# Attention score matmuls of 16 heads on two row halves of TensorE, and the order of the side rounds

## The reference

```python
qkv = (x @ w_qkv).reshape(b, s, 3, 16, 16)            # 16 heads of width 16
q, k, v = jnp.moveaxis(qkv, 2, 0)
attn = softmax(einsum('bqhd,bkhd->bhqk', q, k) * 16 ** -0.5)
x = layernorm(x + einsum('bhqk,bkhd->bqhd', attn, v).reshape(b, s, d) @ w_proj + b_proj)
# mixture of 8 experts, top 2, capacity 5120 rows: x -> (gelu(x W1a) * (x W1b)) W2, gated, summed by token
x = layernorm(x + experts(x))
```

## Time and profile before

| | us |
|---|---|
| median of 3 runs | 3741.0 (3740.78 to 3743.41) |
| profiled execution, its span | 3738.5 |
| PE busy | 3498.9 (94%) |
| DVE busy | 2507.9 (67%) |
| ACT busy | 2007.2 (54%) |
| POOL busy | 1171.2 (31%) |

### The profile page before, as it was taken

How to read it: one execution, slowest core, us unless ns; L and a number is a source line. 1 busy time by engine, 2 the same in 40 slices (tenths; PEclk the granted TensorE clock), 3 DMA queues, 4 the chain that set the end, 5 groups by cost and what they waited for, 6 DMA issues and landing times. The chain is left out here.

```text
span 3738.5 us, 68180 instructions
## 1 busy us (share of the span) xinstructions
PE 3498.9 (94%) x19714; PEld 2455.3 (66%) x19714; DVE 2507.9 (67%) x5866; ACT 2007.2 (54%) x3877; POOL 1171.2 (31%) x929
## 2 busy tenths in 40 slices
PE   5999999999999999999999968999999999999970
PEld 3555565555555555555556537888888888888860
DVE  6787787777778778778777745455555545454539
ACT  2666666666666666666666653444444444444420
POOL 3013213122131231221312233343444535353334
PEclk8999999999999999999999989999999999999985
DMA  6777777756565555555555624444434443443439
GB/s 114 153 156 158 167 151 172 128 92 106 87 107 93 93 105 88 95 104 92 106 91 91 105 71 78 62 75 69 63 64 63 74 64 62 60 68 50 57 56 337
DMA packets 410259, 376.39 MB, mean 101 GB/s; under 512 B 249528, under 2 KB 311360, under 8 KB 409920
## 3 DMA queue, kind: packets, MB, share of 16 engines
q1 hardware_dynamic: 346944, 287.82, 41.5%
q0 software_dynamic: 58368, 67.74, 11.5%
q10 hardware_dynamic: 4608, 16.78, 1.1%
HBM read 89.92 MB, written 152.17 MB: 65 GB/s over the span
## 5 line engine op out<-in xcount | busy, mean ns | idle before, releaser
L880 DVE TENSOR_REDUCE peak<-ps_rows 128x1 f32<-128x512 f32 x2048 | 1349.7, 681 | 477.8 <-PE ps_rows L557 460.9
L648 ACT ACTIVATE probs<-ps_cols 128x512 f32<-128x512 f32 x2048 | 1120.5, 600 | 378.5 <-PE ps_cols L566 375.2
L557 PE MATMUL ps_rows<-stack 128*128 128x512 f32 x2048 | 893.8, 438 | 46.5 <-issue 33.3
L1088 PE MATMUL ps_hid<-x_hi,stack 128*128 128x512 f32 x2560 | 804.6, 395 | 33.0 <-DVE x_lo L1181 28.4
L566 PE MATMUL ps_cols<-stack 128*128 128x512 f32 x2048 | 813.1, 398 | 2.3 <-ACT probs L648 1.9
L1058 POOL DMA_INDIRECT x<-out,token x320 | 503.6, 1574 | 797.7 <-ACT out L1144 657.6
L1187 DVE TENSOR_TENSOR hid<-ps_hid,act_in 128x512 f32<-128x512 f32 x320 | 218.8, 688 | 599.0 <-ACT act_in L1130 598.8
L557 PEld LDWEIGHTS ps_rows<-stack 128*128 128x128 f32 x2048 | 389.6, 190 | 309.7 <-DVE peak L880 213.5
L1088 PEld LDWEIGHTS ps_hid<-x_hi,stack 128*128 128x128 f32 x2560 | 476.6, 189 | 142.5 <-DVE x_lo L1181 28.5
L579 PE MATMUL ps_pv<-probs,v 128*17 128x512 f32 x4096 | 545.1, 604 | 0.9 <-ACT probs L648 0.9
L423 POOL TENSOR_SCALAR var_eps<-mv 128x4 f32<-128x4 f32 x32 | 7.5, 234 | 1593.9 <-DVE mv L752 1593.9
(11 more groups left out here) (130 smaller groups left out, 3575.5 us busy)
## 6 DMA issues: line engine op xcount, KB each, us to landing
stack<-qk_hi SPq DMA_DIRECT2D x512, 128.0 KB
stack<-qk_lo SPq DMA_DIRECT2D x512, 128.0 KB
expert_rows<-blank SPq DMA_DIRECT2D x80, 520.0 KB, 5.0
quarters<-expert_rows SPq DMA_DIRECT2D x320, 128.0 KB, 2.7
xs<-in_L_attn_x SPq DMA_DIRECT2D x32, 512.0 KB, 3.4
x<-row SPq DMA_DIRECT2D x32, 512.0 KB
fy<-x SPq DMA_DIRECT2D x32, 512.0 KB, 4.7
out<-fz ACTq DMA_DIRECT2D x32, 512.0 KB, 4.9
```

What stands on the lines that cost most here:

```text
L557: pe.matmul(ps_rows[n % ROWS][:], q_stack[s][:, h, t * P:(t + 1) * P], k_stack[s][:, h, :], start=True, stop=True).then_inc(s_rows, 1)
L648: act.activation(probs[:, j % RING, :], ps_cols[j % 2][:], ACT.Exp, scale=SCALE).then_inc(s_exp, 1)
L880: dve.tensor_reduce(peak[s % 2][:, j:j + 1], ps_rows[n % ROWS][:], AX.X, ALU.max, negate=True).then_inc(s_max, 1)
L1088: last = pe.matmul(ps_hid[f % 2][:, part, :], w[c.par][:, k, cols], xx[c.odd][:, k, :], start=i == 0, stop=i == 3 * KT - 1)
```

## The change

The score operands lie in two row halves of 64 rows: even heads in one, odd heads in the other. Each half holds three terms (the lo.lo product is dropped), 48 rows, and two rows for the maxima. A unit's row score reads one half and its column score the opposite one. The four units between two pv now follow each other: all rounds stand directly behind a pv (j = 1, 5, 9, 13), several of them in one place where needed. DVE's side work is moved to match.

```diff
-STACK = 4 * HD
+TERMS = 3
+STACK = TERMS * HD
 AUG = 2
+HALF = P // 2
+PAIRS = HG // 2
 ROUNDS = [
-    (0, 1, "x1T0", -2), (0, 3, "x1T1", -2), (0, 5, "peak3", -1), (0, 7, "turn1", -1), (0, 9, "xT0", 1),
-    (0, 11, "logit", -2), (0, 13, "xT1", 1), (0, 15, "logitT", -2),
-    (1, 3, "qk0", 1), (1, 5, "peak0", 0), (1, 7, "turn2", -1), (1, 11, "qk1", 1), (1, 15, "qk2", 1),
-    (2, 1, "place", -2), (2, 3, "qk3", 1), (2, 5, "peak1", 0), (2, 7, "turn3", -1), (2, 11, "oT0", -1), (2, 13, "oT1", -1),
-    (2, 15, "proj0", -1),
-    (3, 3, "proj1", -1), (3, 5, "peak2", 0), (3, 7, "turn0", 0), (3, 11, "v0", 1), (3, 15, "v1", 1),
+    (0, 1, "xT0", 1), (0, 1, "xT1", 1), (0, 5, "peak3", -1), (0, 5, "turn1", -1), (0, 9, "x1T0", -2),
+    (0, 9, "x1T1", -2), (0, 13, "logit", -2),
+    (1, 1, "logitT", -2), (1, 1, "qk0", 1), (1, 5, "peak0", 0), (1, 5, "turn2", -1), (1, 9, "qk1", 1), (1, 13, "qk2", 1),
+    (2, 1, "place", -2), (2, 1, "qk3", 1), (2, 5, "peak1", 0), (2, 5, "turn3", -1), (2, 9, "v0", 1), (2, 13, "oT0", -1),
+    (2, 13, "oT1", -1),
+    (3, 1, "proj0", -1), (3, 5, "peak2", 0), (3, 5, "turn0", 0), (3, 9, "proj1", -1), (3, 13, "v1", 1),
 ]
+def rows_unit(j):
+    return 1 - j % 2, j // (2 * TILES), j % (2 * TILES) // 2
...
-                        for r, (a, c) in enumerate([(hi, hi), (lo, hi), (hi, lo), (lo, lo)]):
-                            rows = slice(HD * r, HD * r + HD)
...
-                        sp.dma_start(q_stack[g][STACK:STACK + AUG].bitcast(F32), zero_rows[:]).then_inc(s_stack[g], 16)
+                        for half_ in range(2):
+                            part = slice(first + half_ * (GP // 2), first + (half_ + 1) * (GP // 2))
+                            for r, (a, c) in enumerate([(hi, hi), (lo, hi), (hi, lo)]):
+                                rows = slice(HALF * half_ + HD * r, HALF * half_ + HD * (r + 1))
...
-                        sp.dma_start(q_stack[g][STACK:STACK + AUG].bitcast(F32), peak_rows[g % 2][:]).then_inc(s_aug[g], 16)
+                        for half_ in range(2):
+                            rows = slice(HALF * half_ + STACK, HALF * half_ + STACK + AUG)
+                            sp.dma_start(q_stack[g][rows].bitcast(F32),
+                                         peak_rows[g % 2][half_ * UNITS:(half_ + 1) * UNITS]).then_inc(s_aug[g], 16)
...
-                            pe.matmul(ps_rows[n % ROWS][:], q_stack[s][:, h, t * P:(t + 1) * P],
-                                      k_stack[s][:, h, :], start=True, stop=True).then_inc(s_rows, 1)
+                            half_, h, t = rows_unit(j)
+                            part = slice(HALF * half_, HALF * half_ + STACK)
+                            pe.matmul(ps_rows[n % ROWS][:], q_stack[s][part, h, t * P:(t + 1) * P],
+                                      k_stack[s][part, h, :], start=True, stop=True).then_inc(s_rows, 1)
...
-                            pe.matmul(ps_cols[j % 2][:], k_stack[g][:, h, t * P:(t + 1) * P], q_stack[g][:, h, :],
+                            t, h, half_ = j // HG, j % HG // 2, j % 2
+                            part = slice(HALF * half_, HALF * half_ + STACK + AUG)
+                            pe.matmul(ps_cols[j % 2][:], k_stack[g][part, h, t * P:(t + 1) * P], q_stack[g][part, h, :],
                                       start=True, stop=True).then_inc(s_cols, 1)
...
-                        if j:
-                            empty(s, j - 1)
+                        for name in AT[s, j - 1] if j else []:
+                            empty(name)
...
-                        if j in (8, 9) and it.on(-1 if s < 3 else 0):
-                            (turn_sums if j == 8 else turn)(f"turn{(s + 1) % 4}", (s + 1) % 4)
-                        low = {(1, 5): 0, (1, 13): 1, (2, 0): 2, (2, 5): 3}
+                        if j in (6, 7) and it.on(-1 if s < 3 else 0):
+                            (turn_sums if j == 6 else turn)(f"turn{(s + 1) % 4}", (s + 1) % 4)
+                        low = {(1, 3): 0, (1, 11): 1, (1, 15): 2, (2, 3): 3}
...
-                        if it.on(1) and s == 0 and j in (11, 15):
-                            low_x((j - 11) // 4)
+                        if it.on(1) and s == 0 and j in (3, 4):
+                            low_x(j - 3)
```

More of the change, by code:

```diff
@@ L63 @@
 OFFSET = {r[2]: r[3] for r in ROUNDS}
-AT = {(r[0], r[1]): r[2] for r in ROUNDS}
+AT = {(s, j): [r[2] for r in ROUNDS if r[:2] == (s, j)] for s in range(4) for j in range(UNITS)}
+def rows_unit(j):
+    return 1 - j % 2, j // (2 * TILES), j % (2 * TILES) // 2
 def wait(engine, sem, value):
@@ L155, with __init__ @@
 class Weights:
-    def __init__(self, stacks, probs, w1, w2):
+    def __init__(self, stacks, w2_buf, probs, w1, w2):
         flat = [stack[:].rearrange("p h n -> p (h n)") for stack in stacks]
         half = FT * DIM
-        self.w1_hi, self.w1_lo = [[flat[i + j].rearrange("p (k f) -> p k f", k=KT) for j in range(2)] for i in (0, 2)]
-        self.w2_hi, self.w2_lo = [[flat[4 + j][:, i * half:(i + 1) * half].rearrange("p (k d) -> p k d", k=FT)
+        self.w1_hi, self.w1_lo = [[flat[i + j:i + j + KT] for j in (0, 2 * KT)] for i in (0, KT)]
+        self.w2_hi, self.w2_lo = [[w2_buf[:, 2 * j + i].rearrange("p (k d) -> p k d", k=FT)
                                    for j in range(2)] for i in range(2)]
@@ L402, in _ @@
             for g in range(GROUPS):
[L404 to L413, removed]
+                for half_ in range(2):
+                    rows = slice(HALF * half_ + 32, HALF * half_ + HALF)
+                    if g + half_ == 0:
+                        pool.wait_ge(s_blank, 2)
+                    else:
+                        pool.wait_ge(s_pad, 2 * g + half_)
+                    pool.memset(k_stack[g][rows].bitcast(F32), 1.0).then_inc(s_pad, 1)
+            pool.wait_ge(s_pad, 2 * GROUPS)
             pool.wait_ge(s_weights, 64)
@@ L581, in body @@
                                 last.then_inc(s_pv, 1)
-                        name = AT.get((s, j))
-                        if name and it.on(OFFSET[name]):
-                            round_(it, name)
+                        for name in AT[s, j]:
+                            if it.on(OFFSET[name]):
+                                round_(it, name)
             iterations(pe, n_seq, body)
@@ L598, in copy_out, with empty @@
                     act.copy(out, in_).then_inc(s_free[it.bank(name)], 1)
-                def empty(s, j):
-                    name = AT.get((s, j))
-                    if name and it.on(OFFSET[name]):
+                def empty(name):
+                    if it.on(OFFSET[name]):
                         ps_m = ps_round[it.bank(name)]
@@ L663, in _ @@
         def _(dve):
-            dve.memset(gate_t[:], 0.0)
-            dve.memset(zero_rows[:], 0.0).then_inc(s_zero, 1)
+            dve.memset(gate_t[:], 0.0).then_inc(s_zero, 1)
             dve.wait_ge(s_weights, 64)
@@ L883, in body @@
                         if j in (1, 2) and it.on(off):
-                            parts = peak_parts[g % 2]
+                            parts = peak_parts[g % 2][:].rearrange("p (a r u) -> p a r u", a=2, r=AUG)
+                            heads = peak[g % 2][:].rearrange("p (a u) -> p a u", a=2)
                             if j == 1:
@@ L1087, in hidden @@
                         for w, xx in ((w1_hi, x_hi), (w1_lo, x_hi), (w1_hi, x_lo)):
-                            last = pe.matmul(ps_hid[f % 2][:, part, :], w[c.par][:, k, cols], xx[c.odd][:, k, :],
+                            last = pe.matmul(ps_hid[f % 2][:, part, :], w[c.par][k][:, cols], xx[c.odd][:, k, :],
                                              start=i == 0, stop=i == 3 * KT - 1)
@@ L1346, in transformer_layer @@
     with ExitStack() as ctx:
-        stacks = [ctx.enter_context(nc.sbuf_tensor(f"stack{i}", [P, HG, SEQ], F32R)) for i in range(2 * GROUPS)]
+        stacks = [ctx.enter_context(nc.sbuf_tensor(f"stack{i}", [P, PAIRS, SEQ], F32R)) for i in range(2 * GROUPS)]
+        w2_buf = ctx.enter_context(nc.sbuf_tensor("w2_buf", [P, 4, FT * DIM], F32R))
         probs = ctx.enter_context(nc.sbuf_tensor("probs", [P, RING, SEQ], F32))
-        weights = Weights(stacks, probs, w1, w2)
+        weights = Weights(stacks, w2_buf, probs, w1, w2)
         attention(nc, x, w_qkv, w_proj, b_proj, w_gate, x1, table, stacks, probs, weights)
```

51 lines of the change are left out of this document (24 added, 27 removed).

## The result

The changed kernel takes 3920.9 us (median of 4 runs, 3919.6 to 3922.8) beside 3742.2 (4 runs, 3740.8 to 3747.7) of the kernel before on the same chip: 1.0477 times as long, 95% interval 1.0464 to 1.0489. It is slower by 179 us. The profiled execution spans 3920.0 us.

What follows compares the result with a forecast made beforehand. PE was taken to set the pace in attention, DVE next. 2.1 + 1.8 + 1.2 + 0.7 = +5.8 us per sequence, times 31.5 is +183; heads -7, start +2, tail +2: +180, 3920 us, range 3800 to 4050.

Steps and rivals of the forecast that it cites:

- The run's length: Run of four units: first exp to pv takes 1.61 us however fast the scores; +0.35 per qk block, +0.30 per turn.
- Logit: Logit round directly behind pv in the same tile shape: loses both switches, gets the longer run; 0.
- turn1: Round turn1 waits for the bank that the second low part of x frees on DVE: +0.7 us per sequence.
- two v rounds taken alike: Blocks of rounds v0 and v1: lengthen as the four qk blocks do, +0.35 each, +2.1 for all six.
- The pair's head: Gap of some 2.6 us ending each pair of iterations: ACT catches up in it, 15 x -0.5 = -7 us.
- Start and tail: Kernel's ends: three more load issues before the first group, +2 us; the columns-only tail, +2 us.
- A third switch: Scores, pv and rounds now have three tile shapes: 0.2 us per switch, hidden where ACT's copy leads (qk, v).
- A: Rival: row halves don't overlap in the score matmuls; +1.5 us per sequence more, 3970 us; chance 0.18.
- C: Rival: no change; copies hidden, switch free, column score together with row score; 3740 us; chance 0.05.
- D: Rival: PE's idle waits halve the granted clock in each turn block, 7 us per sequence; 4130 us; chance 0.08.
- B: Rival: faster, as PE's time is the limit and falls; 56 us a sequence, 3435 us; chance 0.12.
- Signs: Changed profile, if right: "place" starts 71 to 72 us apart, PE well under 90%, DVE near 72%.

Runs made afterwards that it cites:

- the half exp: Changed kernel with ACT's exp of the scores over the first 256 of 512 columns only: 3765.0 us, ratio 1.0079 against the kernel before.
- the early low parts: Changed kernel with DVE's low parts of x one unit earlier, behind units 2 and 3 of stage 0: 3889.6 us, ratio 1.0410 against the kernel before.

## Right and wrong, step by step

The sign, the cause and the size held: 3920 was predicted, 3920.9 came. That it came within 1 us is luck: two errors cancelled in it. Blocks by their rounds, from the starts of pv between the place rounds 1010.73 and 1076.47 before and 1085.43 and 1156.45 after, us per sequence inside a pair:

| blocks | before | after | measured | predicted |
|---|---|---|---|---|
| four qk (after: logitT with qk0) | 17.70 | 19.25 | +1.55 | +1.4 |
| two v | 8.83 | 9.92 | +1.09 | +0.7 |
| four turn | 13.96 | 15.55 | +1.59 | +1.2 and 0.7 for turn1 |
| the rest: xT, x1T, oT, proj, logit | 25.24 | 26.30 | +1.06 | +1.8 |
| sum | 65.73 | 71.02 | +5.29 | +5.8 |

- **The run's length.** 1.61 was read from the logitT run and stood at 1.56 to 1.59 in 14 of the 16 runs of the sequence in the table (1.66 in qk3's, 2.01 in v1's, of which more below). qk blocks 4.73 and 4.74 (+0.32 for +0.35), turns 3.76 (+0.27 for +0.30), the xT block 4.23 for 4.27, x1T and oT 4.22 for 4.29. A little of qk's excess is logitT, which now lies in qk0's block (4.91), and the place round, now directly ahead of qk3 (4.87). This was right, and the half exp shows the cause: the exp chain, not PE. (A third bank for the column scores, which would loosen the same chain, was not tried.)
- **Logit.** Taken at 0. Its block is 3.55 now. Before, xT0 and logit shared one of 4.19, of which 0.42 was xT0's; that leaves 3.77. The loss of two switches was named and not priced: -0.2. Together with the double transposed blocks (12.67 for 12.85) and logitT, whose round took 0.3 of a block of this row before and now stands in qk0's row of the table, this makes the rest's difference, +1.06 for +1.8.
- **turn1.** Taken at 0.7; inside a pair its block is 0.48 longer than another turn's, with a wait of 0.26 at its transposes:

```profile
978.90 0.68 DVE L734 TENSOR_TENSOR x_t_lo<-ps_round,x_t_hi 128x512 fp32r<-128x512 f32 x1
...
979.63 0.66 PE L511 MATMUL ps_round<-ident,pv 128*128 128x128 f32 x4 [0.26 <-DVE x_t_lo L734]
```

The low part ends at 979.58 and the transposes start at 979.63. The place was right and the size too high inside a pair; at the head of a pair the wait is 0.84, and the early low parts show what it costs in all: 26 us, near 31.5 x 0.7 = 22, though some waits at the heads stay.
- **v1.** The step "two v rounds taken alike" held for v0 (4.75 for 4.40) and failed for v1: 5.17 for 4.43, +0.74. It overlooked the border of iterations, where three banks and 64 units meet in one bank. `n % ROWS` stood in the code. No run changes the ring, but with half an exp v1's block keeps its length (5.16) while v0's falls to 4.33, as a wait for DVE and not for ACT would have it.
- **The pair's head.** Taken at -0.5 for each pair, since ACT would catch up in the gap. Over 27 intervals, from the place rounds' first and 28th start, a sequence costs (2183.38 - 209.67) / 27 = 73.10 where it cost (2024.52 - 200.32) / 27 = 67.56: +5.54. With +5.3 inside the pair, the one across a border grew by 5.8 on average, so the head gives +0.5 in place of -0.5. Yet the catching up is real, and larger than taken. Windows view of one border of the kernel before, then two of the changed kernel:

```profile
266.05:334.38 68.33, 65.99 (x380) 39.50 (x377) 52.40 (x133) 44.15 (x86) 16.36 (x15) 1.00 0.74 159
280.63:352.21 71.58, 65.67 (x380) 32.54 (x377) 51.60 (x133) 44.34 (x86) 16.42 (x15) 1.00 0.44 136
1009.24:1085.43 76.19, 69.72 (x381) 34.89 (x377) 52.80 (x133) 44.53 (x86) 16.40 (x15) 0.93 0.26 72
```

Where the clock stays at 1.00, a border takes 2.60 more than an interval inside a pair before, and only 0.56 more after. What the prediction left out is the clock. In the changed kernel 12 of the 13 borders have stretches at half clock, 3.4 to 13.7 us in all; before, 8 of 13 had one, of 3.4. An estimate from these intervals: borders exceed an inner interval by 4.3 on average after and by 3.8 before; less the 0.56 and 2.60, the clock, with the waits that come only where it falls, costs 3.7 and 1.2, so 2.5 more for each pair, some 33 of the 179 us. At the border shown above the blocks of v1, xT, turn1 and x1T last 5.80, 5.39, 6.48 and 5.43, for 5.17, 4.23, 4.25 and 4.22 inside a pair: little is lost at the gap itself, and most behind it, to longer waits and to two stretches of half clock (timeline; windows view):

```profile
1053.55 1.11 PE L511 MATMUL ps_round<-ident,pv 128*128 128x128 f32 x4 [0.84 <-DVE x_t_lo L734]
```

```profile
1046.40:1049.60 3.20, 3.20 (x17) 2.40 (x13) 1.51 (x4) 2.92 (x6) 3.20 (x3) 0.50 0.30 74
1053.20:1059.90 6.70, 6.35 (x24) 3.21 (x25) 3.81 (x8) 2.17 (x4) 5.18 (x6) 0.50 0.55 190
```

Ahead of the first stretch stands PE's wait of 1.62 us at 1044.58; no run isolates what brought the clock down. The two errors cancel: two sequences were to cost 2 x 5.8 - 0.5 = 11.1 more, and cost 2 x 5.54 = 11.1 more.
- **Start and tail.** The first place round comes 9.35 us later and the time behind the 28th grows by 22.6; 27 x 5.54 + 9.35 + 22.6 = 181.5, the difference of the two spans (3920.0 - 3738.5). Predicted were 2 for the start and 2 for the tail, with 31.5 sequences; 4.5 of these lie in the two ends, 25 us, which leaves 7 for both against 4.
- **A third switch.** Last round matmul to first score is 1077.22 to 1077.55 = 0.33, 0.10 above a spacing, as taken.
- **Rivals.** A (halves one behind the other) is false: both start at 1077.55. C is false. D holds for the head of a pair only: 0.97 in the window, above the 0.95 named; its share there was priced above at some 33 us. B (faster) was wrong for this kernel by the point it named, 1.57 against 0.9, and right about the operands: with rounds between the pairs they gain 3 to 3.5%. The Trainium skill, TensorEngine Tiling, Theoretical Speedup, gives up to 2 times for contractions of at most 64: PE's pair of scores does take 0.24 in place of 0.46 us here (second row score at 1077.88, third at 1078.12), and the kernel gains only as far as exps run beside something.
- **Signs.** "Place" starts stand 71.02 apart inside a pair, as said, but 73.1 on average. DVE is busy 71% of 600 to 1500 us, as said; PE 91.5%, not well under 90%.

Not predicted was the best version. The halves in the old order beat both kernels, by 3% against the kernel before. From their undisturbed blocks (qk 3.90 for 4.42, turn 3.33 for 3.50) more could be had than that; how much of it the stalls and the clock of 0.93 took on those chips was not separated, since this version was not run on the chip without stalls. Left open too is the changed kernel's own time on a chip with stalls.

## What to carry to other kernels

When a wait such as "column score j waits for exp j-2" costs nothing, ask what stands between the two; work that is regrouped takes that cover away, and the chain behind it (here copy, exp, exp, pv: 1.6 us) then sets the time however fast the matmuls get. Price the run as a chain through all its engines before pricing the engine that the windows view calls the bound, and look at borders of iterations, where a ring that does not divide the count meets itself. When a change bundles an operand form and an order, try them apart: here the form alone made the kernel 3 to 3.5% faster, the order alone 4% slower, and both together 4.8% slower (the first two on other chips than the third, each against the kernel before on its own chip).

## What the runs showed of the hardware

- Matmuls on opposite row halves start together (1077.55 and 1077.55) and run at full length each (0.50 and 0.49): the overlap is complete, not staggered by 0.11 as was taken.
- Short waits alone left the clock where it was: the changed kernel's stretch from 280.63 to 352.21, with its waits for exps, ran at 1.00. Behind the longer wait at the head of each pair (1.4 to 2.1 us, and up to 0.84 ahead of turn1) the time at half clock was 3.4 to 13.7 us in 12 of 13 cases, where it was 3.4 in 8 of 13 before, behind gaps of 2.3 to 2.9.
- Chips differed by 5% on the same kernel (3738.6, 3918.1 and 3938.4 us). On the slower two, traces of other kernels show idle times of 1 us and more ascribed to issue on PE and to "remote" on ACT at heads of iterations, where the first had one gap of 2.6 for each pair. A time from one chip can't be set beside one from another.
